# Layer 0 scan: diagonals of B for all sixteen states, in place of scaled copies and transposes for six

## The reference

```python
def step(h, inp):
    dt_l, u_l, B_l, C_l = inp
    dA = jnp.exp(dt_l[..., None] * A)
    h = h * dA + (dt_l * u_l)[..., None] * B_l[:, :, None, :]
    y = jnp.einsum('bkdn,bkn->bkd', h, C_l)
    return (h, y)
```

## Time and profile before

| | us |
|---|---|
| median of 3 runs | 9207.98 (9200.64 to 9214.95) |
| time of the profiled execution | 9207.24 |
| its span, first to last instruction | 9205.4 |
| mean granted TensorE clock | 0.921 of full |

### The profile page before, as it was taken

The page is one execution under the profiler, slowest core; times in us unless marked ns, Lnnn a source line. Parts: engine busy times, 40 slices in busy tenths (PEclk is TensorE's granted clock), DMA queues, the critical chain, the costliest instruction groups (busy, mean ns, idle before and its releaser), DMA issues. The chain is left out here.

```text
span 9205.4 us, 142734 instructions
## 1 busy us (share of the span) xinstructions
PE 7794.9 (85%) x50982; PEld 6018.6 (65%) x50982; DVE 5517.8 (60%) x8186; ACT 3754.6 (41%) x7820; POOL 3974.0 (43%) x2456
## 2 busy tenths in 40 slices
PE   8999799989999899953355556688879999999999
PEld 6888588867887688841355553345656666666666
DVE  7999799979999799952233335556662222222222
ACT  6787488747876588720011112203431111111111
POOL 5888388847887488820488880031000000000000
PEclk9999999999999999975677778789999999999999
DMA  2333133312332133322455550000002222222221
GB/s 65 91 91 88 50 91 91 89 58 81 90 90 80 58 90 91 88 100 66 117 159 157 157 158 21 3 0 2 0 7 95 92 86 82 76 99 92 86 92 71
DMA packets 461971, 736.07 MB, mean 80 GB/s; under 512 B 46319, under 2 KB 366984, under 8 KB 459569
## 3 DMA queue, kind: packets, MB, share of 16 engines
q1 hardware_dynamic: 409649, 560.19, 19.4%
q0 software_dynamic: 51840, 169.91, 6.3%
HBM read 707.51 MB, written 43.72 MB: 82 GB/s over the span
## 5 line engine op out<-in xcount | busy, mean ns | idle before, releaser
L591 POOL TENSOR_TENSOR l_arena<-l_arena 128x768 f32<-128x768 f32 x1536 | 2778.6, 1824 | 470.6 <-DVE l_arena L541 408.5
L541 DVE TENSOR_TENSOR_SCAN l_arena<-l_arena,psum 128x384 f32<-128x384 f32 x3072 | 2867.9, 984 | 77.0 <-PE psum L382 41.7
L475 ACT ACTIVATE l_arena<-l_arena,l_A 128x384 f32<-128x384 f32 x3072 | 1665.3, 604 | 81.7 <-DVE l_arena L541 81.6
L384 PE MATMUL psum<-l_arena 128*128 128x128 f32 x11520 | 1579.8, 284 | 28.8 <-DVE l_arena L541 25.1
L384 PEld LDWEIGHTS psum<-l_arena 128*128 128x128 f32 x11520 | 1405.7, 192 | 185.4 <-issue 114.6
L395 PE MATMUL psum<-l_ident,l_arena 128*128 128x128 f32 x9216 | 1259.7, 273 | 53.1 <-ACT l_yT L481 45.5
L1963 DVE TENSOR_TENSOR st_Uc<-psum,st_both 128x384 f32<-128x384 f32 x512 | 285.5, 558 | 1699.8 <-PE psum L1884 1699.8
L976 POOL DMA_INDIRECT l_G<-neighbourhoods,l_idc x648 | 879.6, 1357 | 699.6 <-issue 690.4
L395 PEld LDWEIGHTS psum<-l_ident,l_arena 128*128 128x128 f32 x9216 | 1053.5, 141 | 64.3 <-POOL l_arena L591 41.5
L1884 PE MATMUL psum<-st_F,st_xt 128*128 128x384 f16 (+2 forms) x6912 | 1002.1, 290 | 0.0
L995 PE MATMUL psum<-l_ident,l_G 128*128 128x128 f32 x2592 | 450.2, 356 | 534.9 <-DVE l_G L959 534.9
(11 more groups left out here) (326 smaller groups left out, 7729.2 us busy)
## 6 DMA issues: line engine op xcount, KB each, us to landing
l_arena<-c_rows SPq DMA_DIRECT2D x1536, 192.0 KB, 3.0
st_FS<-filter_sums SPq DMA_DIRECT2D x128, 641.0 KB, 7.4
st_F<-filter_parts SPq DMA_DIRECT2D x128, 576.5 KB, 6.1
neighbourhoods<-padded_image SPq DMA_DIRECT2D x16, 1300.5 KB
st_mab<-in_st_mp SPq DMA_DIRECT2D x68, 256.0 KB, 7.4
st_mab<-in_st_mm SPq DMA_DIRECT2D x68, 256.0 KB, 7.7
l_G<-neighbourhoods,l_idc POOLq DMA_INDIRECT x648, 3.6
l_gnx<-in_x SPq DMA_DIRECT2D x4, 1152.0 KB, 5.6
```

What stands on the lines that cost most here:

```text
L384: mm = pe.matmul(ps[:, o:o + P], dtuT[:, g % 2, t, h * P:(h + 1) * P], diagB[:, rank[s] % 3, t, :], start=True, stop=True)
L475: act.activation(decay[:, s % NDC, h, :], dtv[:, g % 2, h, :], ACT.Exp, scale=A[:, g // NRC, h, n:n + 1]).then_inc(s_exp, 1)
L541: dve.tensor_tensor_scan(hbuf[:, n, h, flip], decay[:, s % NDC, h, flip], ps[:, BANK * (2 * (s % 2) + h):BANK * (2 * (s % 2) + h) + RC][:, ...
L591: pool.tensor_tensor(hC[:, s % NHC], hbuf[:, s % NS], Cs[:, s % NCS, :].unsqueeze(1).broadcast_to([P, 2, RC]), ALU.mult).then_inc(s_hc, 1)
```

## The change

The six states in TURNED no longer get a scaled copy of dtuT and a transpose. ScalarE now makes `diagA`, the three diagonals of B for the state, from the identity matrix `ident` (128 columns each where the copies had 256), in a ring of two; `make_input` runs the same product with dtuT for every state, with `diagA` or `diagB` at its right. `turned_input` no longer waits for dtuT (semaphore s_tc), which it doesn't read now. `diagA` takes the first half of the space that `xT` had. Line numbers in the diff are those of the kernel before.

```diff
--- before.py
+++ after.py
@@ -115,7 +115,7 @@
         dtv, dtu = (cut(12288 + 1536 * i, 4 * RC).rearrange("p (r h l) -> p r h l", r=2, h=2) for i in range(2))
         dtuT = cut(15360, 4 * RC).rearrange("p (r t d) -> p r t d", r=2, t=LB)
         soft = cut(16896, 2 * RC).rearrange("p (h l) -> p h l", h=2)
-        xT = cut(17664, 4 * RC).rearrange("p (r t d) -> p r t d", r=2, t=LB)
+        diagA = cut(17664, 2 * RC).rearrange("p (r t l) -> p r t l", r=2, t=LB)
         diagB = cut(19200, 3 * RC).rearrange("p (r t l) -> p r t l", r=3, t=LB)
         decay = cut(20352, NDC * 2 * RC).rearrange("p (r h l) -> p r h l", r=NDC, h=2)
         hC = cut(23424, NHC * 2 * RC).rearrange("p (r h l) -> p r h l", r=NHC, h=2)
@@ -376,13 +376,10 @@
                         for h in range(2):
                             if s >= 2:
                                 pe.wait_ge(s_scan, 2 * (s - 2) + h + 1)
+                            turned_B = diagA[:, rank[s] % 2] if n in TURNED else diagB[:, rank[s] % 3]
                             for t in range(LB):
                                 o = BANK * (2 * (s % 2) + h) + t * P
-                                if n in TURNED:
-                                    mm = pe.transpose(ps[:, o:o + P], xT[:, rank[s] % 2, t, h * P:(h + 1) * P], ident[:])
-                                else:
-                                    mm = pe.matmul(ps[:, o:o + P], dtuT[:, g % 2, t, h * P:(h + 1) * P], diagB[:, rank[s] % 3, t, :],
-                                                   start=True, stop=True)
+                                mm = pe.matmul(ps[:, o:o + P], dtuT[:, g % 2, t, h * P:(h + 1) * P], turned_B[:, t, :], start=True, stop=True)
                             mm.then_inc(s_x2, 1)
 
                     def sum_states(s):
@@ -458,11 +455,10 @@
                     def turned_input(s):
                         n, g, i = s % NS, s // NS, rank[s]
                         act.wait_ge(s_bt, g + 1)
-                        act.wait_ge(s_tc, 2 * g + 2)
                         if i >= 2:
                             act.wait_ge(s_x2, 2 * turned[i - 2] + 2)
                         for t in range(LB):
-                            ins = act.activation(xT[:, i % 2, t, :], dtuT[:, g % 2, t, :], ACT.Copy, scale=BT[:, g % 2, t, n:n + 1])
+                            ins = act.activation(diagA[:, i % 2, t, :], ident[:], ACT.Copy, scale=BT[:, g % 2, t, n:n + 1])
                         ins.then_inc(s_xT, 1)
 
                     def decays(s):
```

## The result

The changed kernel takes 9424.53 us (median of 4 runs, 9415.39 to 9426.93) against 9210.75 for the kernel before, with its repeats. The ratio is 1.0232, 95% interval 1.0214 to 1.025: slower by 214 us. The forecast was 9401, slower, with a range of 9325 to 9470.

A forecast was written before the change was run, and what follows sets the result against it. VectorE was taken to set the pace, TensorE nearly level; the change makes TensorE pacemaker. Per scan +47.8 to the last but one chunk, +0.8 there, 0 in the last: +48.6, for four +194; 9207.2 + 194 = 9401 us, range 9325 to 9470.

The forecast's parts named there:

- The price of a turned state: On TensorE, six turned states a chunk become straight, 6 x (1.34 - 0.65) = 4.1 us more; bounds 3.9 and 4.3.
- two short groups might pay a fresh fill: Upper bound for TensorE's added passes: two short groups per chunk cost another 0.1 us each, 4.3 us in all.
- The y wait: TensorE's 1.2 us wait for ScalarE to copy y out, hidden before, now paid in 12 chunks a scan.
- The first chunk: A scan's first chunk sums only 13 states and has no y wait: 36.5 - 3 x 0.66 = 34.5 us.
- The sum: From L338 of a scan's first chunk to that of the last but one: 829.7 us against 781.9, +47.8.
- ScalarE and the dropped wait at nothing: ScalarE's narrower copies (185 us less work) and the dropped wait on s_tc were both costed at nothing.
- Idle time before the scans: VectorE's idle time before L541 rises from 77 us to about 260 us, all put down to TensorE.
- TensorE's waits for scans: Short waits of TensorE's products (L384) for VectorE's scans (L541), 1.25 us a chunk before, were to shrink.
- The stretch of a scan: One scan of layer 0 grows from 860 to about 909 us.
- the rival on weight loads: TensorE's weight loads are the resource: 725 of a scan's 860 us grow by 211 to 936; +304, 9511 us; chance 3%.
- is all that separates TensorE from VectorE: TensorE's short waits for scans, 1.25 us of a 34.88 us chunk, were read as its whole distance from VectorE.
- the strided L338: Where the next direction reads columns strided, L338 takes 2.75 against 1.49 us and the chunk 36.97 against 35.70.

The follow-up runs named there:

- the y copy first: Kernel before, with ScalarE's copy of y out of PSUM issued ahead of the softplus piece: 9189.13 us, ratio 0.9977.
- The run with the copy first: Changed kernel, with ScalarE's copy of y out of PSUM issued ahead of the softplus piece: 9369.09 us, ratio 1.0171 to the kernel before.
- the run with doubled transposes: Kernel before, with each transpose of the six turned states issued twice into the same place: 9401.54 us, ratio 1.0206.
- state 12: Kernel before, with only state 12 made with a diagonal, the other five turned states unchanged: ratio 1.0008.
- state 2: Kernel before, with only state 2 made with a diagonal, the other five turned states unchanged: ratio 1.0069.
- eight turned states: Kernel before, with eight states (2, 3, 5, 7, 9, 11, 13, 15) as scaled copies and transposes, not six: 9142.07 us, ratio 0.9922.
- its opposite: Kernel before, with eight states as scaled copies and transposes, not six, and the y copy issued ahead of the softplus piece: 9112.1 us, ratio 0.989.

## Why the prediction was right

The step that carries it held: TensorE's passes, counted by starts of groups, set the length of every chunk once six turned groups become straight. Its parts:

- *The price of a turned state.* Taken as 4.1 us a chunk, bounded by 3.9 and 4.3. Measured 3 x (1.34 - 0.65) + 3 x (1.45 - 0.71) = 4.3: the three groups behind a projection pay a longer start as products too. This was the upper bound, and "two short groups might pay a fresh fill" was three. That accounts for 0.13 to 0.23 us a chunk between forecast and measurement, about 4 us a scan.
- *The y wait.* 2.55 us from product to sum in both kernels, of which 1.2 are the wait: hidden before, but for the 22 us that the y copy first gave there, and paid now. The run with the copy first took out 56 us of the forecast's 12 x 1.2 x 4 = 58.
- *The first chunk.* I took three sums off; only two of the three missing sums lie between the two starts of L338. Forecast 34.5, measured 135.05 - 99.63 = 35.42 us.
- *The sum.* 829.7 us forecast between the first and the last but one L338, 834.3 measured. With the tail, a scan from its first L338 to the end of the last addition grew from 854.7 to 907.8 us, 53.1, so 212 us for four, against 194. Of the two spans' difference (207.2) that leaves -5 us outside these stretches, no more than runs of one kernel differ.
- *ScalarE and the dropped wait at nothing.* For ScalarE's narrower copies it is shown: 1.0001. The dropped wait was in no run by itself; ScalarE's own copy of dtu stands ahead of it in program order, and the sums above leave nothing for it.
- *Idle time before the scans* rose to 239 us; 260 was forecast.
- *TensorE's waits for scans.* Forecast to shrink; the list of waits has none now.
- *The stretch of a scan.* "From 860 to about 909 us" was the forecast; 53.1 us more make it 913.

Two readings that the sum didn't rest on were poor. First, the rival on weight loads (936 us a scan). It added 211 us of single loads to a busy time of 725, but busy time counts overlapping loads once: 18432 loads of 192 ns are 3539 us and the row shows 2187. The stretch has 814.9 us of loads, 89.3%. The trace of before gave it away, with 11520 loads of 192 ns (2212 us) in 1405.7 us of busy time. The Trainium skill's page "Perfetto Trace Analysis", section "Identifying the Most-Contended Engine", would have TensorE's headroom judged by the share of its weight loads. With overlapping loads counted once, as the profile's rows count, that share leaves it a tenth; the page writes it as the sum of the loads' times over the window, and then the products and sums alone are over the window, (18432 x 192 + 9216 x 141) ns / 4 = 1210 of 912 us. Neither tells what is left: the starts show no headroom in this kernel. In the run with doubled transposes the loads are 140 ns in place of 192, fill 806.7 of 907 us (88.9%), and its chunks are as long to within 0.9%, so the length of a load can be worth no more than that. In this case the measurement decides against that measure: distances between starts told what TensorE had left.

Second, I wrote that 1.25 us a chunk of short waits "is all that separates TensorE from VectorE". As a total that is so. As a reserve it isn't: it can be used in states 9 to 15 (state 12, +8 us) and not behind L338 (state 2, +62 us). For six states at once the totals decide, which is why the sum came out; for a smaller change of the same kind the same reasoning would have forecast zero where 62 us are paid. What was already in the rows, the strided L338 whose 1.27 us were paid in full, pointed that way. I read it as the two engines being nearly level, but the two chunks compared are late ones of 35.70 and 36.97 us, in which TensorE, by my own sum of 32.4 us, had over 3 us to spare: it was paid for its place.

Left open: why a product group behind a projection takes 0.1 us longer than one behind a sum. No run was made on it. Every pass in these runs has one weight load, so whether the load or the matmul sets the 0.11 us of a pass is open too. Nor was it tried whether more than eight turned states pay.

## What to carry to other kernels

Where two engines hand work back and forth and both are over nine tenths busy, compare their costs per period by the distances between starts, not by busy time, and then ask at which point of the period each is ahead: in this kernel an operation put where the other engine waits was paid in full (62 us), and one put where the other leads was nearly free (8 us). A wait hidden by the pacemaker has to be added to the sum as soon as the pace moves to the engine that holds it. And when an exchange turns out to cost, its opposite is worth a run: here it gave 1.1% with one list of states and two statements swapped.

## What I had not expected

A single state's diagonal, 0.73 us of TensorE work a chunk on an engine with 2.5 us of waits in it, cost 0.73 us everywhere, and the other one 0.69 us nowhere but in two chunks. Also the start of a group: in the same kernel the same twelve passes take 1.34 us behind a sum and 1.45 behind L338, and six transposes 0.65 and 0.71.
